# One block for the constants, the edge sort and the scatter of a graph network kernel, with places of 16 columns beside the scatter

## The reference

```python
def _L0_gnn_ref(node_input, node_attr, edge_src, edge_dst, edge_attr, edge_scalars, w_lin1_s, w_lin1_v, fc_w1, fc_w2, ...):
    s = s @ (w_lin1_s / jnp.sqrt(jnp.float32(MUL)))
    v = jnp.einsum('nui,uw->nwi', v, w_lin1_v / jnp.sqrt(jnp.float32(MUL)))
    h = jax.nn.silu(edge_scalars @ (fc_w1 / ...)) * SILU_NORM
    w = h @ (fc_w2 / ...)
    ...
    ns = jax.ops.segment_sum(mid_scal, edge_dst, num_segments=N) * inv
    ...
x = _layernorm(x + _L0_gnn_ref(...))
x = _layernorm(x + _L1_gnn_ref(...))   # four convolutions, summed by dst
x = _layernorm(x + _L2_gnn_ref(...))   # mean over neighbours, summed by src
x = _layernorm(x + _L3_gnn_ref(...))   # attention, by dst
```

## Time and profile before

| | before |
|---|---|
| median of 3 runs | 8487.9 us |
| lowest, highest | 8483.14, 8493.29 us |
| the profiled execution | 8494.57 us |
| its span | 8492.8 us |
| instructions | 105,913 |

### The profile page before, as it was taken

How to read it: one execution, slowest core, us unless ns; L and a number is a source line. 1 busy time by engine, 2 the same in 40 slices (tenths; PEclk the granted TensorE clock), 3 DMA queues, 4 the chain that set the end, 5 groups by cost and what they waited for, 6 DMA issues and landing times. The chain is left out here.

```text
span 8492.8 us, 105913 instructions
## 1 busy us (share of the span) xinstructions
PE 5666.3 (67%) x23206; PEld 3954.1 (47%) x23206; DVE 5705.7 (67%) x15407; ACT 3353.5 (39%) x10636; POOL 6043.0 (71%) x6427
## 2 busy tenths in 40 slices
PE   5777747667666666676676776666655555788885
PEld 3444424444444444444444443444444444666664
DVE  8959148888666666666666666555544444788887
ACT  3333347777455553433323332000001111566665
POOL 2777767776577777777777776777777777666664
PEclk6555557777788888999989998888865555788886
DMA  2111144344222224444344444544433322111111
GB/s 75 59 58 59 58 120 113 111 112 111 77 64 64 63 63 128 119 119 119 111 146 119 119 118 133 122 116 116 116 89 62 62 62 60 50 49 49 49 49 38
DMA packets 632226, 749.12 MB, mean 88 GB/s; under 512 B 257061, under 2 KB 490169, under 8 KB 631465
## 3 DMA queue, kind: packets, MB, share of 16 engines
q0 software_dynamic: 239808, 572.66, 23.6%
q1 hardware_dynamic: 391512, 169.55, 7.9%
q10 hardware_dynamic: 272, 0.14, 0.0%
HBM read 617.05 MB, written 124.77 MB: 87 GB/s over the span
## 5 line engine op out<-in xcount | busy, mean ns | idle before, releaser
L824 DVE TENSOR_TENSOR acc<-acc,ps 128x256 f32 (+3 forms) x4704 | 1762.2, 375 | 1632.7 <-PE ps L1866 1245.6
L1149 POOL DMA_INDIRECT rows<-table_gcn,index_dst x1984 | 1890.1, 953 | 671.8 <-issue 574.6
L1866 PE MATMUL ps<-rows,hot 128*128 128x256 f32 (+2 forms) x5536 | 1517.4, 411 | 1229.9 <-DMA rows<-table_gcn,index_dst 495.4
L1866 PEld LDWEIGHTS ps<-rows,hot 128*128 128x128 f32 x5536 | 1110.2, 248 | 1631.0 <-issue 700.4
L1760 ACT ACTIVATE ut<-u,fld 128x128 f16<-128x128 f16 x1568 | 541.8, 392 | 1533.4 <-DVE u L1808 1532.8
L1149 POOL DMA_INDIRECT rows<-table_gat,index_dst x832 | 784.8, 943 | 375.3 <-issue 238.8
L1149 POOL DMA_INDIRECT rows<-table_lin,index_dst x784 | 739.8, 944 | 302.3 <-issue 231.9
L1149 POOL DMA_INDIRECT rows<-table_mean,index_src x784 | 741.2, 945 | 249.3 <-issue 230.2
L1118 PE MATMUL ps<-prod,hot 128*128 128x257 f32 x1568 | 635.6, 543 | 394.2 <-DVE prod L1071 313.3
L1851 PE MATMUL ps<-prod,ut 128*128 128x392 f16 x3136 | 738.3, 364 | 0.5 <-ACT ut L1760 0.5
L1149 POOL DMA_INDIRECT hot_v<-table_gcn,index_dst x576 | 547.9, 951 | 175.5 <-issue 166.7
(11 more groups left out here) (429 smaller groups left out, 11086.0 us busy)
## 6 DMA issues: line engine op xcount, KB each, us to landing
fld<-dst_rows SPq DMA_DIRECT2D x98, 544.0 KB, 4.2
rows<-table_gcn,index_dst POOLq DMA_INDIRECT x1984
table_gcn<-acc SPq DMA_DIRECT2D x147, 128.0 KB
fld<-left_rows SPq DMA_DIRECT2D x147, 128.0 KB
pay<-dst_rows SPq DMA_DIRECT2D x832, 1.0 KB
rows<-table_gat,index_dst POOLq DMA_INDIRECT x832
rows<-table_lin,index_dst POOLq DMA_INDIRECT x784
rows<-table_mean,index_src POOLq DMA_INDIRECT x784
```

Source lines behind the costliest of these rows:

```text
L824: c.nc.vector.tensor_tensor(to, to, product, ALU.add).then_inc(c.added.sem, 1)
L1149: pool.indirect_dma_start(to(q, j), None, table, bass.IndirectOffsetOnAxis(ap=c.idx[k][:, t:t + 1], axis=0)).then_inc(c.gathered[q % per]. ...
L1866: pe.matmul(c.ps[:, bank(q, j), 0:used], c.hot[:, r % 2, j, :], row_of(c, s, r, j, used), start=True, stop=True).then_inc(c.mm.sem, 1)
```

## The change

`setup`, `sort_dst`, `prepare_weights` and `scatter_dst` become one block, `place_edges`.

- DVE only counts the destination bins (`count_dst`): 25 marks whose sums are written by `accum_out`, with no scan, no predicated copy and no positions. Field writes come before `bins_ranked`, which is the old ranking. The mark writes to two buffers in turn.
- `locate` replaces `positions` for the destination. It takes 8, 48 times 16, and 6 columns (`DCUTS`). It compares with all bins, laid out bin by bin with the columns innermost, in two PSUM banks (6 and 7); it scans each half with a row of resets that is zero at each bin's first column; it multiplies by `dst_both`, adds the running base of each bin, sums the products over the bins with a step of n columns, and writes the new base back (`base`).
- The weights are scaled behind the fifth cut (`ready_weights`), fc1 and fc2 apart and first (`scale_fc`). `ranked` for the destination comes after the last cut; its matmuls stand on PE behind turn 44. The source sort (`scan_src`, the old rounds) follows; its matmuls stand behind turn 54. The source places keep cuts of 32 columns.
- The node product moves into turns 44 to 94, one bin a turn, in bank 7, and its rows are stored four bins at a time.
- The loads are put in another order: destination keys, fc1, fc2, edge scalars, source keys, edge vectors, the other weights, x.
- The positions' fill, payload buffer and constants are cleared on POOL (`constants`); DVE clears only tails, weights and the reset rows.

```diff
-CUT = (0, 8, 24, 48) + tuple(range(48 + MAXCUT, TC, MAXCUT)) + (TC,)
+CUT = tuple(range(0, TC, MAXCUT)) + (TC,)
 NCUTS = len(CUT) - 1
-EARLY = 4
+DCUT = 16
+DCUTS = (0, 8) + tuple(range(8 + DCUT, TC, DCUT)) + (TC,)
+NDCUTS = len(DCUTS) - 1
+SORT = (4, 5, 5, 6)
+TABLES, LISTED, ONE = 5, 304, 460
+VALUE, HOT = 112, 6
+NODES = 7
+NODES_FROM = 44
+SHELF = 4
+WEIGHTS_BEHIND = 4
...
+def count_dst(c, s, dve):
+    st = Steps(dve, c.dve)
+    dve.wait_ge(s.key_loaded["dst"].sem, s.key_loaded["dst"].n + 32)
+    halves_of_key(c, s, dve, "dst")
+    masks = (s.mask, s.run)
+    for b in range(NB // 2):
+        if b >= 2:
+            st.wait(but=1)
+        st(dve.scalar_tensor_tensor(in_halves(masks[b % 2]), in_halves(s.pair), float(b), s.value, ALU.is_equal, ALU.mult,
+                                    accum_out=s.nch[:, b:b + 1]))
+    st.wait()
+    two_counts(c, s, dve)
+    fields_of_key(c, s, dve, "dst")
+    dve.wait_ge(s.key_loaded["src"].sem, s.key_loaded["src"].n + 32)
+    fields(c, s, dve, "src", "dst", s.ends[:, :, 0], s.ends[:, :, 1])
+    dve.wait_ge(c.dve.sem, c.dve.n)
+    dve.sem_inc(s.ends_ready.sem, 1)
...
+def locate(c, s, dve, cut):
+    t, n = DCUTS[cut], DCUTS[cut + 1] - DCUTS[cut]
+    st = Steps(dve, c.dve)
+    bins, base, wide = sort_rows(c, SORT)
+    halves = lambda ap: ap.rearrange("p (a e) -> p a e", a=2)
+    hot = c.ps[:, HOT:HOT + 2, 0:NB // 2 * n]
+    area = lambda i: s.tab[:, i * DCUT * NB:i * DCUT * NB + n * NB]
+    run_, one_, two_ = area(0), area(1), area(2)
+    run = run_.rearrange("p (b t) -> p b t", t=n)
+    columns = lambda row: row.unsqueeze(2).broadcast_to([P, NB, n])
+    in_banks = lambda ap: ap.rearrange("p (a b) t -> p a b t", a=2)
+    as_bins = lambda ap: ap.rearrange("p a (b t) -> p a b t", t=n)
+    by_column = lambda ap: ap.rearrange("p (b t) -> p t b", t=n)
+    small = lambda i, of=1: s.tab[:, 3 * DCUT * NB + i * DCUT:3 * DCUT * NB + (i + of) * DCUT]
+    low, both, both_i = small(0)[:, 0:n], small(1)[:, 0:n], small(2).bitcast(I32)[:, 0:n]
+    parts_i = small(4, 2).bitcast(I32).rearrange("p (a t) -> p a t", a=2)[:, :, 0:n]
+    parts = small(6, 2).rearrange("p (a t) -> p a t", a=2)[:, :, 0:n]
+    past, step, place = small(8)[:, 0:n], small(9)[:, 0:n], small(10)[:, 0:n]
+    st(dve.tensor_tensor(as_bins(hot), in_banks(s.binf[:, t:t + n].unsqueeze(1).broadcast_to([P, NB, n])),
+                         in_banks(columns(bins)), ALU.is_equal)).wait()
+    for a in range(2):
+        st(dve.tensor_tensor_scan(halves(run_)[:, a, :], halves(s.reset[n])[:, a, :], hot[:, a, :], 0.0, ALU.mult, ALU.add))
+    st(dve.tensor_tensor(as_bins(halves(two_)), as_bins(hot), in_banks(columns(s.dst_both)), ALU.mult)).wait(but=1)
+    st(dve.tensor_tensor(run, run, columns(base), ALU.add)).wait(but=1)
+    st(dve.tensor_reduce(both, by_column(two_), AX.X, ALU.add)).wait(but=1)
+    st(dve.tensor_tensor(halves(one_), halves(run_), hot, ALU.mult)).wait(but=1)
+    st(dve.tensor_copy(both_i, both)).wait(but=1)
+    st(dve.tensor_reduce(low, by_column(one_), AX.X, ALU.add)).wait(but=1)
+    st(dve.tensor_scalar(parts_i[:, 0, :], both_i, SPLIT_BITS, None, ALU.arith_shift_right))
+    st(dve.tensor_scalar(parts_i[:, 1, :], both_i, int(SPLIT) - 1, None, ALU.bitwise_and)).wait()
+    st(dve.tensor_scalar(past, low, -1.0, None, ALU.add))
+    st(dve.tensor_copy(parts, parts_i)).wait()
+    st(dve.scalar_tensor_tensor(step, parts[:, 0, :], float(P), parts[:, 1, :], ALU.mult, ALU.subtract))
+    st(dve.tensor_tensor(place, past, parts[:, 1, :], ALU.add)).wait(but=1)
+    st(dve.scalar_tensor_tensor(step, past, 0.0, step, ALU.is_lt, ALU.mult)).wait()
+    dve.tensor_tensor(s.pos_i[:, t:t + n], place, step, ALU.add).then_inc(s.located.sem, 1)
+    st(dve.tensor_copy(base, run[:, :, n - 1])).wait()
...
+            def edge_scalars(q):
                 if q >= 2:
                     sp.wait_ge(m.h_mm.sem, m.h_mm.n + 2 * (q - 1))
                 sp.dma_start(s.ea8[:, q % 2, 0:size(q) * P if q < SCG else E - SCG * G8 * P],
                              A["ea8"][:, q * G8 * P:min((q + 1) * G8 * P, E)]).then_inc(m.ea[q % 2].sem, 16)
+            def store(g):
+                n = min(NB, (g + 1) * SHELF)
+                sp.wait_ge(m.taken.sem, m.taken.n + n)
+                sp.dma_start(tiles(table, NB, D)[:, g * SHELF:n, :], shelf(g)[:, 0:n - g * SHELF, :]
+                             ).then_inc(m.shelf[g % 2].sem, 16)
+            sp.dma_start(s.key["dst"][:, 0:TC - 1], A["dst_main"]).then_inc(s.key_loaded["dst"].sem, 16)
+            sp.wait_ge(s.tails.sem, 1)
+            sp.dma_start(s.key["dst"][0:TAIL, TC - 1:TC], A["dst_tail"]).then_inc(s.key_loaded["dst"].sem, 16)
+            sp.dma_start(s.fc1[:, :], A["L0_gnn_fc_w1"]).then_inc(s.fc_loaded.sem, 16)
+            sp.dma_start(s.fc2[:, :], A["L0_gnn_fc_w2"]).then_inc(s.fc_loaded.sem, 16)
+            edge_scalars(0)
+            edge_scalars(1)
+            sp.wait_ge(s.tails.sem, 3)
+            sp.dma_start(s.key["src"][:, 0:TC - 1], A["src_main"]).then_inc(s.key_loaded["src"].sem, 16)
+            sp.dma_start(s.key["src"][0:TAIL, TC - 1:TC], A["src_tail"]).then_inc(s.key_loaded["src"].sem, 16)
+            sp.dma_start(s.attr[:, 0:TC - 1, :], A["ea4_main"]).then_inc(s.attr_loaded.sem, 16)
+            sp.dma_start(s.attr[0:TAIL, TC - 1, :], A["ea4_tail"]).then_inc(s.attr_loaded.sem, 16)
+            edge_scalars(2)
+            sp.wait_ge(s.tails.sem, 6)
+            for dst, src in s.first_weights:
+                sp.dma_start(dst, src).then_inc(s.x_loaded.sem, 16)
+            for dst, src in s.weights:
+                sp.dma_start(dst, src).then_inc(c.load.sem, 16)
+            sp.dma_start(c.x[:, 0:NT - 1, :], tiles(A["x"][0:(NT - 1) * P, :], NT - 1, D)).then_inc(s.x_loaded.sem, 16)
+            sp.dma_start(c.x[0:LASTN, NT - 1, :], A["x"][(NT - 1) * P:N, :]).then_inc(s.x_loaded.sem, 16)
+            for q in range(3, turns):
+                edge_scalars(q)
+                g = q - NODES_FROM - 5
+                if g >= 0 and g % SHELF == SHELF - 1:
+                    store(g // SHELF)
+            for g in range((turns - NODES_FROM - 5) // SHELF, shelves):
+                store(g)
+            for h in range(2):
+                sp.wait_ge(m.shelf[h].sem, m.shelf[h].n + 16 * ((shelves + 1 - h) // 2))
...
+            pe.wait_ge(s.fc_scaled.sem, s.fc_scaled.n + 1)
             hidden(0)
             for q in range(turns):
                 if q + 1 < turns:
                     hidden(q + 1)
                 weights(q)
-                if q == RING:
-                    ranked_pe(c, s, pe, "dst", 0, (4, 5, 6, 7))
-                if q == SCG // 2:
-                    sort_pe(c, s, pe, "src", (4, 5, 6, 7))
-                    ranked_pe(c, s, pe, "src", 1, (4, 5, 6, 7))
+                if q == 0:
+                    sort_pe(c, s, pe, "dst", SORT)
+                if q == NODES_FROM:
+                    ranked_pe(c, s, pe, "dst", 0, SORT)
+                if q == NODES_FROM + 10:
+                    sort_pe(c, s, pe, "src", SORT, 1)
+                    ranked_pe(c, s, pe, "src", 1, SORT)
+                if 0 <= q - NODES_FROM <= NB:
+                    node(q - NODES_FROM)
...
+            clear_tails(c, s, dve)
+            bins_known(c, s, dve)
+            scale_fc(c, s, dve)
+            count_dst(c, s, dve)
+            bins_ranked(c, s, dve, "dst", SORT)
+            for cut in range(NDCUTS):
+                locate(c, s, dve, cut)
+                if cut == WEIGHTS_BEHIND:
+                    ready_weights(c, s, dve)
+            ranked(c, s, dve, "dst", 0, SORT)
+            scan_src(c, s, dve)
+            bins_ranked(c, s, dve, "src", SORT, 1)
+            ranked(c, s, dve, "src", 1, SORT)
             for cut in range(NCUTS):
-                positions(c, s, dve, "dst", cut, (4, 5, 6, 7))
-                if cut == EARLY - 1:
-                    ranked(c, s, dve, "dst", 0, (4, 5, 6, 7))
-            sort_dve(c, s, dve, "src", (4, 5, 6, 7))
-            ranked(c, s, dve, "src", 1, (4, 5, 6, 7))
-            for cut in range(NCUTS):
-                positions(c, s, dve, "src", cut, (4, 5, 6, 7))
+                positions(c, s, dve, cut)
...
+            act.wait_ge(s.unused_ready.sem, s.unused_ready.n + 1)
+            act.dma_start(tiles(s.dst_rows[TC * P:NCH * P, :], NCH - TC, PW), s.unused[:, :, :]
+                          ).then_inc(s.prefilled.sem, 16)
             silu(0)
+            act.wait_ge(s.pay_cleared.sem, s.pay_cleared.n + 1)
+            act.wait_ge(s.attr_loaded.sem, s.attr_loaded.n + 32)
+            act.wait_ge(s.ends_ready.sem, s.ends_ready.n + 1)
             for q in range(turns):
                 if q + 1 < turns:
                     silu(q + 1)
                 payload(q)
+                if q == 2:
+                    act.wait_ge(c.load.sem, c.load.n + 16 * len(s.weights))
```

(62 more changed lines are left out.)

366 lines of the change are left out of this document (144 added, 222 removed).

## The result

The changed kernel takes 8447.85 us (median of 4 runs, 8441.89 to 8448.54) beside 8489.8 us of the kernel before, a ratio of 0.9944 (95% interval 0.9932 to 0.9957): 42 us less, where 86 were forecast. The time lies 7 us above the range, and the interval leaves no doubt that the kernel got faster. The profiled execution took 8448.16 us with a span of 8446.4.

What follows compares the result with a forecast made beforehand. POOL's indirect-DMA scatters bound the changed stage after an idle lead-in. Starting 94 us earlier, less an 8 us stall at turn 54, gives -86 us: 8487.9 - 86 = 8402 us, range 8388 to 8441.

Steps and rivals of the forecast that it cites:

- The lead-in: Stretch before POOL's first scatter: that scatter starts at 50 us instead of 144.3, a gain of 94 us.
- Count loop: DVE's 25 destination masks: start at 8.1 us (bounds 7 and 11), 1.05 us a round, 26.3 us in all.
- The covers: Moved loads, weights' scaling, node product and POOL's new holds: hidden behind other work, costing nothing by themselves.
- the price of places: DVE's destination cuts: 8.9 us per 16 columns, against 20.3 us that POOL takes to scatter them.
- the 6 us to spare at turn 44: PE's first wait for DVE's lists: payload 45 at 501.6, wanted by POOL at 507.7, so no stall.
- rival B: DVE's cuts take 9.4 to 9.8 us because of short rows and PSUM; time 8412 to 8445 us, chance 0.15.
- rival C: Strided reads in the cuts pay 1.04 ns an element, 1.66 us a cut; time 8482 us, chance 0.04.
- Payload 45: ScalarE's payload behind PE's first wait: ready at 501.6, after DVE at 488.4 plus 12.3 and 0.9 us.
- The second gap: POOL's stall at turn 54, behind the source sort: payload 55 at 617.7, wanted at 609.4, 8 us.
- D: Slower kernel: three or more large passes per cut take two element times, 2.5 us a cut; 8520 us, chance 0.04.

Runs made afterwards that it cites:

- The probe: Changed kernel plus VectorE sums and products of various steps in an idle stretch, each issued three times on its own line; 27 SBUF reductions took 36.50 us together.
- the turned version: Changed kernel with both products of a cut written column by column, step 50 floats, so the sums read in sequence; ratio 0.9964 to the kernel before.
- in place: Changed kernel with each cut's second product written over the one-hot in PSUM and summed there; 8429.49 us, ratio 0.9925 to the kernel before.

## Why the prediction was wrong

**The lead-in was right.** Count loop from 8.1 forecast, from 9.71 measured. L241 and its two followers, all small, end only at 6.8, which is when GpSimd's two memsets of the payload buffers (2.99 to 6.74) end; whether these held them wasn't tried. The 1.6 us lie within the bounds. A round took 0.89 us, not 1.05: the accumulator's read-out is an instruction of its own of 0.08 us (L285), and the next mark starts with it, at 10.61. 22.4 us for 25, inside the bounds of 21.5 and 28. Ranking began at 37.30 and ended at 42.18, 4.9 us. First scatter 49.03, forecast 50.

**The covers held.** Weights, x, scaling, holds and node product left no gap on GpSimd: the trace has none but the two, and the experiments put these down to the waits.

**The failed step is the price of places**, "with 0.1 for the odd slow small operation, 8.9 us per 16 columns". It was 9.78 over 48 cuts, the weights' 4.4 us taken out. The two sums cost 1.48 and 1.49 instead of 0.98, 1.0 us more, and the small operations 0.1 less. The error is 48 x 0.88 = 42 us. It used up the 6 us to spare at turn 44, which the prediction had as "no stall", and it came through undiluted, as rival B said ("each 0.1 us per cut is 4.8 us of end"): the first list matmul at 529.55 for a forecast 488.4, the second at 646.58 for 604.5, the last scatter at 1092.13 for 1051.2. In the span that is 8446.4 for 8492.8 - 86 = 8406.7. The other 6 us of the 46 between forecast and measured time come from the profiled executions: that of before lay 6.7 us above the median, that of after 0.3.

**How it came about.** For the stepped read I took L1071's row, 584 ns for 384 elements with a step of 128 bytes, and read "at most 0.07 ns an element more". That is a little low: with the fixed part of 0.15 us taken off both rows it is 0.10, or 0.08 us a pass, which is still small. The row was right and didn't match the case. It sums three elements at a time and starts the next sum one float further, so that its three lines are used four times over. The probe reproduces it (1.06 us for 768, L748) and shows that with four lines the price is there in full (1.48, L749). The cut's sums walk over 50 lines. A row of the same operation with the same step isn't the nearest row if the order in which it comes back to its lines differs.

**The rule.** The Trainium skill (SBUF — State Buffer, "Door 1: The DMA port swizzle") has each access to a new line pay, and (Advanced Engine Details and Errata, "SBUF Cachelines") needs at least two hits on a line to absorb the latency. Within one sum the runs agree with both: a step of 2 floats is free (1.01 us), a step of 4 pays (1.59). From sum to sum they don't follow the words: sums over 3 change the line at each access and pay next to nothing (1.06), and lines that two sums touch once each still pay a half (1.30). I had set the rule aside on the strength of the one row and kept it as rival C with 0.04, at a price of one element time (1.04 ns) that no row supported; it is 0.6 ns (1.51 less 1.01 over 800). C's cause with 0.6 of C's price lands in B's place (9.4 to 9.8 us per cut, 8412 to 8445 us), which I had given another cause and 0.15. That the time lies so near B's band is therefore no merit of B's reasons: the products and the addition, with rows of 16 and most with PSUM on one side, took their 0.97 to 0.98 us. My range ended at 8441, inside that band. With the price of a new line between nothing and one element time as its bounds, the range would have reached 8482.

**The two gaps.** Payload 45 was there at 542.3 (forecast 501.6), 12.9 us after the end of VectorE's last operation before the lists (forecast 13.2), and wanted at 503.5 (forecast 507.7, for the steps before it took 1.26 us and not 1.271): hence 39.6 us where I had 6 to spare. The second gap was forecast as 8 us and is 11.84. After the first gap the scatter runs late as well, so the second no longer depends on the cut: 11.83 in the turned version and 11.83 in place. It comes from another sum than the forecast 8, and that the two lie near each other is chance. The end follows VectorE and where the waits stand. Moving the source sort brought the last scatter forward by 10 us, moving both waits by 40, and taking 0.4 us out of each cut by 22.

**The slower rival** D would have needed 10.7 us per cut. The changed kernel's cut has neither a stepped write (0.68 us) nor more than its two stepped reads; the turned version, with both products written by step, came to about 10.1.

## What to carry to other kernels

When work is moved off the path to run beside it, look for the places in another engine's in-order queue that wait for it, and compute when each side arrives: the wait's place can be worth as much as the work itself (the lists three turns later and the source sort six gave 30 and 10 us here, with no operation made faster). Price a stepped read in SBUF by how soon it comes back to the same line, not by its step alone. Where a sum must read across, try its operand in PSUM, where the steps tried cost nothing.

## What the runs showed of the hardware

- VectorE, float32, SBUF: a sum's read pays 0.6 to 0.8 ns an element from a step of 4 floats on, no more at 16, and nothing at 2 (1.01, 1.01, 1.59 and 1.51 us for 800 at 1, 2, 4 and 16). Lines touched again in a rotation of up to three are free or nearly so (0.98 and 1.06 us for 768), at four the whole price is due (1.48). A product written with a step of 50 floats costs 0.85 ns an element more (1.69 us beside 1.01). In PSUM the steps tried, 8 and 16 floats, cost nothing (0.60 us for 400 either way; 991 ns for 800 across two banks).
- An accumulated mark (`accum_out`) over 782 elements came every 0.89 us, with its read-out of 0.08 us beside the next mark; the mark alone took 0.944 us on average in the earlier trace rows.
- The granted TensorE clock was 1.00 (2.4 GHz) through the whole scatter of the changed kernel. In the kernel before it was 0.92 in the first 50 us, 0.67 in the next and 0.50 (1.2 GHz) from 100 on, after the burst of the node product from 28 to 72 us; the changed kernel has no such burst, but that the burst brought the clock down wasn't tried. The matmuls of the edge network took 426 and 1,069 ns (L611, L601) at 0.50 and take as long at 1.00, and the node's transposes, 273 ns at the median in the burst (L470), take 422 (L696) at 1.00 beside the scatter. So the granted level did not tell the pace. One stretch of before and one of after (us, busy of PE, PEld, DVE, ACT and POOL, granted clock, DMA share, GB/s), and groups of before (L611, L601) and of after (L681, L671):

```profile
700.00:1090.00 390.00, 280.19 (x769) 161.72 (x768) 179.43 (x242) 129.61 (x532) 296.08 (x309) 0.50 0.17 59
...
700.00:1090.00 390.00, 298.59 (x836) 175.45 (x836) 213.80 (x297) 141.33 (x588) 296.08 (x309) 1.00 0.20 65
```

```profile
L611 PE MATMUL ps<-fc,prod 64*128 64x128 f32 x1536 | 360.4, 426 | 224.5 <-ACT rows L670 114.3 <-ACT pay L670 110.3
L601 PE MATMUL ps<-hot_v,fc 8*64 8x512 f32 x380 | 348.7, 1069 | 0.0
...
L681 PE MATMUL ps<-fc,prod 64*128 64x128 f32 x1353 | 317.9, 426 | 137.6 <-ACT pay L766 68.9 <-ACT rows L766 68.7
L671 PE MATMUL ps<-hot_v,fc 8*64 8x512 f32 x330 | 302.9, 1070 | 0.0
```

What sets the pace instead no run here shows. The stages behind the scatter are as long in both kernels.
